# Gated linear attention and feed-forward on eight cores: the copy of y moved to VectorE, three LayerNorm tiles ahead of the loop

## The chip, the cores and the metric

The kernel runs on the 8 cores of one Trainium2 chip. Each core works on 2,048 of 16,384 tokens, without talking to the others. The metric is the device time of the slowest core in microseconds (us), the median of several runs.

## What is computed

The reference, cut to what matters (B = 1, T = 16384, D = 1024, 16 heads of 64, hidden size 3072):

```python
xn = layernorm(x)
q, k, v = xn @ Wq.T, xn @ Wk.T, xn @ Wv.T     # split in 16 heads
a = sigmoid(xn @ Wg.T)
h_t = a_t[:, None] * h_{t-1} + k_t[:, None] * v_t[None, :]
y_t = q_t @ h_t
x = x + layernorm(y) @ Wo.T
xm = layernorm(x)
x = x + (silu(xm @ wg.T) * (xm @ wu.T)) @ wd.T   # int32 weights / 127
```

## The kernel before

Every core takes its own 2,048 tokens and 256 tokens ahead of them, from which it warms up the state h. The program writes an instruction list for each engine by hand: `O.add("v", ...)` appends to VectorE's list, `"s"` is ScalarE, `"t"` TensorE, `"g"` GpSimd, `"sy"` SyncE, which issues the transposing DMAs. The lists run in order; between engines only the semaphores named in `wait=` hold: TE, VE, SE, GE count the instructions of TensorE, VectorE, ScalarE and GpSimd, the others DMAs (SX loads of x, ST transposes of the normed x, KT and YT transposes of k and y, GX and XQ residual loads and stores). On VectorE, ScalarE and GpSimd each instruction also waits for the one before it on its own engine.

The attention half goes by groups: a warm-up group of 2 tiles of 128 tokens, then four full groups of 4 tiles (8 chunks of 64 tokens). A group has two parts.

- `finish` (lines 385 to 512) projects v (line 406, copied out at 413), runs the second half of the cumulative sums of the log gates (scans, line 435), takes exponentials (443, 446) and projects q and k (475), which line 491 scales.
- `emit_loop` (lines 520 to 778) runs over the chunks, two to a window w. A chunk has the score matmuls (628) into PSUM `p_py`, the mask (641) on VectorE, the state matmuls (651), and `emit_update` (665): lines 667, twice, and 678 on VectorE. At the end of a window TensorE computes y for both chunks (705, 715) into `p_py`. Four copies (731) bring y to `s_y`; SyncE transposes it (744); `emit_update` for the odd chunk follows; then pieces of the next group's front are woven in; then `emit_yln` computes the LayerNorm statistics of y on ScalarE (258 to 277); and `emit_be_late(w - 1)` makes the output projection of the window before (575) with its VectorE work (590, 596, 600, twice each). GpSimd copies half of v across partitions for the next window (557, 561).

The pieces woven in are the `units` that `prep_front` makes for the next group: four LayerNorm tiles on ScalarE (`u_tile`, lines 258 to 284), the transposes (`u_xt`, line 321, four DMAs), eight blocks of the gate projection (`u_gblk`: line 339 on TensorE, 345 and 349 on ScalarE), and the first half of the scans (`u_scan0`, line 360). The table `sched` says how many are taken in each window: 5, 4, 4, 0, and the rest after window 3. The last group has no successor and an empty list. `pyf` holds the count at which a bank of `p_py` is free again.

After the attention half come a second LayerNorm over 16 tiles (lines 845 to 882, transposed at 875 into `s_x2T`), and the feed-forward stage: lines 910 and 923 for gate and up, 949 for down. Line 885 loads all down weights, then line 895 the first gate weights, both on GpSimd's queue.

The table is this line:

```python
sched = {4: [5, 4, 4, 0], 2: [6, 7]}[npair]
```

Of the kernel before, what the change touches and what calls it, by code (L numbers as in the profile page):

```python
# [10 lines left out]
AF = mybir.ActivationFunctionType  # L11
# [6 lines left out]
C = 64  # L18
# [57 lines left out]
def build_program():  # L76
# [73 lines left out]
    ST = _Sem(nc.alloc_semaphore("ST"))  # L150
    KT = _Sem(nc.alloc_semaphore("KT"))
    YT = _Sem(nc.alloc_semaphore("YT"))
    GQ = _Sem(nc.alloc_semaphore("GQ"))
# [5 lines left out]
    VE = _Sem(nc.alloc_semaphore("VE"))  # L159
    SE = _Sem(nc.alloc_semaphore("SE"))  # L160

    O = _Ops()
# [52 lines left out]
    for j in range(8):  # L215
# [4 lines left out]
            wait=([(TE, bw_te)] if j == 0 else ()), inc=VE)  # L220
# [7 lines left out]
    pyf = {0: 0, 1: 0}  # L228
# [4 lines left out]
    G = dict(st_last=0,  # L233
             y_last=0,
             qk_te=0,
             e_wo_te=0,
             fr_se={},
             ln1_se={},
             xr_store={},
             fr_ve={},  # L240
             e_wo_te2=0,
             scan0_ve=0, e0_done=0,
             yt_slot={},
# [48 lines left out]
    def prep_front(tb, nt, wu, gp2):  # L292
# [92 lines left out]
        def finish(dbg_this=False):  # L385
# [7 lines left out]
            def first_use(bk):  # L393
                if bk < 2:
                    return [(VE, pv[0])]
                if bk < 4:
                    return [(SE, pyf[bk - 2])]
                return [(SE, G["fr_se"].get(bk - 4, 0)),
                        (VE, G["fr_ve"].get(bk - 4, 0))]

# [119 lines left out]
    def emit_loop(tb, nt, wu, FR, splice, dbg_this=False):  # L520
# [30 lines left out]
        xr_load(1)  # L551
        if splice:
            splice.loads()
        vsg = {}

        def emit_vs(w2):
# [59 lines left out]
        for cc in range(nch):  # L616
# [7 lines left out]
            if not wu:  # L624
                for h in range(NH):
                    hp, hq = h % 2, h // 2
                    O.add("t", lambda t, w=w, h=h, hp=hp, hq=hq, par=par, cc=cc:
                          t.matmul(
                        p_py[64 * hp:64 * (hp + 1),
                             512 * par + 64 * hq:512 * par + 64 * (hq + 1)],  # L630
                        s_kt[64 * hp:64 * (hp + 1),
                             1024 * w + TILE * hq + C * par:
                             1024 * w + TILE * hq + C * (par + 1)],
                        s_qt[64 * hp:64 * (hp + 1),
                             512 * hq + C * cc:512 * hq + C * (cc + 1)],
                        start=True, stop=True),
                        wait=([(VE, FR["qk_done"]), (SE, pyf[par])]
                              if h == 0 else ()),
                        inc=(TE if h == NH - 1 else None))
                p_mm_done = TE.n  # L640
                O.add("v", lambda v, par=par: v.tensor_tensor(  # L641
                    s_P[:, 512 * par:512 * (par + 1)],
                    p_py[:, 512 * par:512 * (par + 1)],
                    s_mask[:, 512 * par:512 * (par + 1)], ALU.mult),
                    wait=[(TE, p_mm_done)], inc=VE)
                pmask_done = VE.n
# [41 lines left out]
            if (not wu) and par == 1:  # L688
                ug = max(upd_ve.get((gc[0] - 1) % 3, 0),
                         upd_ve.get(gc[0] % 3, 0))  # L690
                for c2 in (cc - 1, cc):
                    par2 = c2 % 2
                    hs2 = (gc[0] - (cc - c2)) % 3
                    for h in range(NH):
                        hp, hq = h % 2, h // 2
                        rhs_v = (
                            (lambda t, c2=c2, hp=hp, h=h:
                             s_V[64 * hp:64 * (hp + 1),
                                 1024 * (c2 // 2) + 64 * h:1024 * (c2 // 2) + 64 * (h + 1)])
                            if hp == par2 else  # L700
                            (lambda t, hp=hp, h=h:
                             s_VS[64 * hp:64 * (hp + 1), 64 * h:64 * (h + 1)])
                        )
                        O.add("t", lambda t, c2=c2, par2=par2, h=h, hp=hp, hq=hq,
                              rhs_v=rhs_v: t.matmul(  # L705
                                  p_py[64 * hp:64 * (hp + 1),
                                       512 * par2 + 64 * hq:512 * par2 + 64 * (hq + 1)],
                                  s_P[64 * hp:64 * (hp + 1),
                                      512 * par2 + 64 * hq:512 * par2 + 64 * (hq + 1)],
                                  rhs_v(t),  # L710
                                  start=True, stop=False),
                              wait=(([(VE, max(pmask_done, ug)), (GE, vs_done)])
                                    if h == 0 else ()))
                        O.add("t", lambda t, c2=c2, par2=par2, h=h, hp=hp, hq=hq,
                              hs2=hs2: t.matmul(  # L715
                                  p_py[64 * hp:64 * (hp + 1),
                                       512 * par2 + 64 * hq:512 * par2 + 64 * (hq + 1)],
                                  s_qt[64 * hp:64 * (hp + 1),
                                       512 * hq + C * c2:512 * hq + C * (c2 + 1)],
                                  s_h[hs2][64 * hp:64 * (hp + 1),  # L720
                                           64 * hq:64 * (hq + 1)],
                                  start=False, stop=True),
                              inc=(TE if (h == NH - 1 and c2 == cc) else None))
                G["y_last"] = TE.n
                vsu[0] = TE.n
                if w + 1 < npair:
                    emit_vs(w + 1)
                for par2 in (0, 1):
                    for hp in (0, 1):
                        O.add("s", lambda s, ysl=ysl, par2=par2, hp=hp:  # L730
                              s.activation(  # L731
                            s_y[64 * par2:64 * (par2 + 1),
                                ysl:ysl + 1024].rearrange(
                                "p (q two o) -> p q two o", two=2, o=C)[:, :, hp, :],
                            p_py[64 * hp:64 * (hp + 1),
                                 512 * par2:512 * (par2 + 1)].rearrange(
                                "p (q o) -> p q o", o=C),
                            AF.Copy),
                            wait=(([(TE, TE.n),
                                    (YT, G["yt_slot"].get(w % 2, 0))])  # L740
                                  if (par2 == 0 and hp == 0) else ()),
                            inc=SE)
                    pyf[par2] = SE.n
                O.dma("sy", YT, lambda sy, w=w, ysl=ysl: sy.dma_start(
                    out=s_E[:].rearrange("p (j q c) -> p j q c",
                                         j=8, q=4, c=TILE)[:, :, w, :],
                    in_=s_y[:, ysl:ysl + 1024].rearrange(
                        "p (j c) -> p j c", j=8),
                    transpose=True),
                    wait=[(SE, SE.n)])  # L750
                yt_eps[w] = O.close_epoch(YT)
                G["yt_slot"][w % 2] = yt_eps[w]
                emit_update()
                if splice:
                    sched = {4: [5, 4, 4, 0], 2: [6, 7]}[npair]
                    for _ in range(min(sched[w], len(splice))):
                        splice.pop(0)()
                yst[w] = emit_yln(w)
                G["yst_slot"][w % 2] = yst[w]
                if w > 0:  # L760
                    emit_be_late(w - 1)
                if splice and w == npair - 1:
                    while splice:
                        splice.pop(0)()
            elif splice and wu and par == 1:
                sched = {2: [6, 7]}[npair]
                for _ in range(min(sched[w], len(splice))):
                    splice.pop(0)()
                if w == npair - 1:
                    while splice:  # L770
                        splice.pop(0)()
# [69 lines left out]
        O.add(eng, fn, wait=w, inc=sem, inc_by=16)  # L841

    a2_done = {}
    ln2q = {}
    for tt in range(16 if TRUNC == 0 else 0):
        buf = tt % 2
        dmaD("g", GX, lambda g, tt=tt, buf=buf: g.dma_start(
# [29 lines left out]
                                   j=8, q=16, c=TILE)[:, :, tt, :],  # L877
            in_=s_a2[:].rearrange("p (j c) -> p j c", j=8), transpose=True),
            wait=[(VE, a2_done[tt])])
        if tt % 4 == 3:  # L880
            ln2q[tt // 4] = O.close_epoch(ST)
    ln2_tp = ST.n

    if TRUNC == 0:
# [8 lines left out]
    for hc in range(NHC if TRUNC == 0 else 0):  # L893
# [10 lines left out]
        gu_ld = O.close_epoch(GQ)  # L904
        for t4 in range(4):
            pb = t4 % 2
            w0 = [(GQ, gu_ld), (ST, ln2q.get(t4, ln2_tp)),
                  (SE, silu_of.get(pb, 0))]
            for j in range(8):
                addD("t", lambda t, buf=buf, t4=t4, j=j, pb=pb: t.matmul(  # L910
                    p_g[pb][:],
# [128 lines left out]
```

How the kernel before makes its waits and increments, by code:

```python
        def run(e, fn=fn, w=w, inc=inc, inc_by=inc_by):  # L56
            for sem, val in w:
                e.wait_ge(sem.h, val)
            ins = fn(e)
            if inc is not None and ins is not None:
                ins.then_inc(inc.h, inc_by)
# [931 lines left out]
        @block.gpsimd  # L993
        def _(g):
            for f in O.q["g"]:
                f(g)
            g.wait_ge(XQ.h, final_xq)
            if final_dq:
                g.wait_ge(DQ.h, final_dq)
```

## Time and profile before

| | |
|---|---|
| runs | 1534.56 and 1540.17 us, median 1537.36 us |
| profiled execution | 1543.56 us, span of its slowest core (core 3) 1542.0 us |
| spans of the eight cores | 1518.9 to 1542.0 us |
| busy in the span | TensorE 956.0 us, VectorE 469.3, ScalarE 368.6, GpSimd 136.2 |
| loops of the four full groups begin at | 285.6, 459.5, 637.6 and 814.3 us |
| second LayerNorm, feed-forward | from 892.9, from 1032.1 us |

The profile is of one execution, times are counted from the first instruction of core 3. Busy time says little here: the attention half is a chain in which engines wait for each other, so the questions are what TensorE waits for, and what stands ahead of that in its queue. Names in the profile are engine, line, output tile and input tiles; a bracket at a row's end is the idle time of the engine ahead of it and what ended it. PE is TensorE, DVE is VectorE, ACT is ScalarE, POOL is GpSimd, SPq the queue of SyncE.

### The profile page before, as it was taken

To read this page: it belongs to the slowest core of one execution; us is meant where nothing else is said; L and a number is where in the kernel's file an instruction comes from. 1 tells how busy PE (TensorE), PEld (TensorE's weight loads), DVE (VectorE), ACT (ScalarE), POOL (GpSimd) and SP (SyncE) were. 2 spreads that over 40 slices of the span, in tenths; PEclk is the share of its full clock that TensorE was granted. 3 is DMA by queue.
4 is the path that set the end of the run, shared out by engine and by line. 5 is a ranking of instruction groups with operands and counts; after the bars stand their busy time and mean duration, and the time that the engine had idled before them with its cause. 6 is when DMAs were issued, how large, how long until landed. Compare 5 with 4: busy or idle time off the path is not lost.

```text
span 1542.0 us, 17776 instructions; the slowest of 8 cores (1518.9 to 1542.0 us)
## 1 busy us (share of the span) xinstructions
PE 956.0 (62%) x5892; PEld 450.5 (29%) x5892; DVE 469.3 (30%) x864; ACT 368.6 (24%) x755; POOL 136.2 (9%) x193
## 2 busy tenths in 40 slices
PE   0115178635762666725675500029999999999997
PEld 0003133313322332413233200004444444444443
DVE  0023235405742266404655534201122111111111
ACT  0032521274106531174203322101111111100000
POOL 2000000101101001001001000001011110101100
PEclk9967576667885777657886755559999999999999
DMA  9902400212201212211103246882444434403232
GB/s 142 164 11 85 78 18 0 36 35 69 99 25 28 63 48 96 35 35 48 63 14 56 68 123 141 149 119 29 41 42 41 39 31 41 55 28 107 93 101 96
DMA packets 144457, 99.98 MB, mean 65 GB/s; under 512 B 123504, under 2 KB 123504, under 8 KB 144368
## 3 DMA queue, kind: packets, MB, share of 16 engines
q0 software_dynamic: 72816, 81.02, 25.6%
q1 hardware_dynamic: 71552, 17.83, 6.5%
q8 instruction: 49, 0.80, 0.2%
q14 instruction: 40, 0.33, 0.1%
HBM read 93.86 MB, written 16.78 MB: 72 GB/s over the span
## 4 chain that ended last, share of the span: by engine, by line
PE 51%; DVE 16%; ACT 11%; DMA 10%; issue 5%; another core or an unknown queue 5%; DVEq 1%; SPq 1%; ACTq 0%; POOL 0%; POOLq 0%
PE p_g L910 11%; PE p_u L923 11%; PE p_d L949 11%; PE p_fr L339 5%; DMA s_x2T<-s_a 4%; PE p_pp L575 3%; DVE s_nL L360 3%; DMA s_wd<-wdi 3%; DVE s_nL L435 3%; PE p_py L475 3%; PE p_fr L475 2%; ACT s_nL L258 2%; ACT s_nL L261 2%; DVE p_pp L590 2%
## 5 line engine op out<-in xcount | busy, mean ns | idle before, releaser
L910 PE MATMUL p_g<-s_x2T,s_wgu 128*128 128x512 bf16 x768 | 183.1, 382 | 149.7 <-DMA s_wgu<-wui 149.7
L923 PE MATMUL p_u<-s_x2T,s_wgu 128*128 128x512 bf16 x768 | 182.4, 381 | 0.0
L339 PE MATMUL p_fr<-s_xlnT,s_wg 128*128 128x512 bf16 (+1 forms) x320 | 83.7, 428 | 146.2 <-ACT s_y L731 82.8
L949 PE MATMUL p_d<-s_wd,s_hff 128*128 128x512 bf16 x768 | 165.9, 379 | 1.2 <-DVE s_hff L929 1.2
L929 DVE SCALAR_TENSOR_TENSOR s_hff<-p_u,s_act 128x512 bf16<-128x512 f32 x96 | 66.4, 692 | 295.6 <-PE p_u L923 295.6
L910 PEld LDWEIGHTS p_g<-s_x2T,s_wgu 128*128 128x128 bf16 x768 | 75.4, 98 | 241.6 <-issue 151.9
L916 ACT ACTIVATE s_act<-p_g 128x512 f32<-128x512 f32 x96 | 57.3, 597 | 271.1 <-PE p_g L910 271.1
L923 PEld LDWEIGHTS p_u<-s_x2T,s_wgu 128*128 128x128 bf16 x768 | 75.4, 98 | 91.7 <-issue 1.9
L949 PEld LDWEIGHTS p_d<-s_wd,s_hff 128*128 128x128 bf16 x768 | 75.1, 98 | 92.0 <-issue 1.7
L339 PEld LDWEIGHTS p_fr<-s_xlnT,s_wg 128*128 128x128 bf16 x320 | 34.7, 113 | 191.6 <-issue 178.1
L575 PE MATMUL p_pp<-s_wo,s_E 128*128 128x512 bf16 x256 | 76.7, 467 | 21.3 <-DVE s_xr L600 21.3
L731 ACT ACTIVATE s_y<-p_py 64x512 bf16<-64x512 f32 x64 | 37.9, 592 | 212.4 <-PE p_py L715 207.1
L590 DVE SCALAR_TENSOR_TENSOR p_pp<-p_pp,s_stats,s_bwB 128x512 f32<-128x512 f32 x32 | 24.3, 758 | 198.8 <-PE p_pp L575 131.8
L705 PE MATMUL p_py<-s_V,s_P 64*64 64x64 bf16 x256 | 29.8, 237 | 80.6 <-DVE s_P L641 80.6
L360 DVE TENSOR_TENSOR_SCAN s_nL<-s_S 128x64 f32<-128x64 bf16 x160 | 46.7, 292 | 69.7 <-ACT s_S L349 52.3
L667 DVE TENSOR_TENSOR s_ht<-p_st,s_h 64x512 f32<-64x512 f32 x72 | 49.6, 688 | 59.2 <-PE p_st L651 51.9
L956 DVE TENSOR_TENSOR s_x<-s_x,p_d 128x1024 f32<-128x1024 f32 x16 | 19.5, 1221 | 148.1 <-PE p_d L949 148.1
L475 PE MATMUL p_py<-s_xlnT,s_wq 128*128 128x512 bf16 x128 | 40.2, 484 | 36.2 <-DVE s_qt L491 36.2
L406 PE MATMUL p_py<-s_wv,s_xlnT 128*128 128x512 bf16 x144 | 42.7, 463 | 22.8 <-DVE s_V L413 22.8
L705 PEld LDWEIGHTS p_py<-s_V,s_P 64*64 64x64 bf16 x256 | 28.2, 151 | 82.1 <-issue 82.1
L183 PE MATMUL p_pp<-s_wo,s_betT 128*1 128x512 bf16 x16 | 4.9, 474 | 72.2 <-DMA s_onec<-ones_c 72.2
L895 POOL DMA_DIRECT2D s_wgu<-wgi x24 | 21.0, 874 | 314.1 <-PE p_u L923 214.4
(109 smaller groups left out, 1137.8 us busy)
## 6 DMA issues: line engine op xcount, KB each, us to landing
s_x<-x2d POOLq DMA_DIRECT2D x32, 512.0 KB, 4.7
s_x<-xs POOLq DMA_DIRECT2D x18, 512.0 KB, 8.8
s_xr<-xs POOLq DMA_DIRECT2D x16, 512.0 KB, 4.5
x2d<-s_xr POOLq DMA_DIRECT2D x16, 512.0 KB, 2.9
out<-s_x POOLq DMA_DIRECT2D x16, 512.0 KB, 3.0
s_wd<-wdi POOLq DMA_DIRECT2D x1, 6144.0 KB, 46.4
s_wgu<-wgi POOLq DMA_DIRECT2D x24, 256.0 KB, 4.5
s_wgu<-wui POOLq DMA_DIRECT2D x24, 256.0 KB, 5.3
```

Of the source, the lines that this page charges most:

```text
L339: O.add("t", lambda t, p=p, j=j, bank=bank: t.matmul(p_fr[bank][:, 0:ntok], s_wg[:, 1024 * j + TILE * p:1024 * j + TILE * (p + 1)], s_xlnT ...
L360: O.add("v", lambda v, cc=cc, p=p: v.tensor_tensor_scan(s_nL[:, 512 * cc + C * p:512 * cc + C * (p + 1)], s_S[:, 512 * p + C * cc:512 * p ...
L475: ntok=ntok: t.matmul(bank6(bank, ntok), s_w[:, 1024 * j + TILE * p:1024 * j + TILE * (p + 1)], s_xlnT[:, 512 * j:512 * j + ntok], start=( ...
L575: O.add("t", lambda t, w=w, j=j, hf=hf: t.matmul(p_pp[hf][:], s_E[:, 512 * j + TILE * w:512 * j + TILE * (w + 1)], s_wo[:, 1024 * j + 512 ...
L590: v.scalar_tensor_tensor(p_pp[hf][:], p_pp[hf][:], r_ap, s_bwB[:, sl], ALU.mult, ALU.add),
L667: O.add("v", lambda v, par=par, hp=hp, hs=hs: v.tensor_tensor(s_ht[64 * hp:64 * (hp + 1), :].rearrange("p (q o) -> p q o", o=C), p_st[64 * ...
L705: rhs_v=rhs_v: t.matmul(p_py[64 * hp:64 * (hp + 1), 512 * par2 + 64 * hq:512 * par2 + 64 * (hq + 1)], s_P[64 * hp:64 * (hp + 1), 512 * par ...
L910: addD("t", lambda t, buf=buf, t4=t4, j=j, pb=pb: t.matmul(p_g[pb][:], s_wgu[buf][:, TILE * j:TILE * (j + 1)], s_x2T[:, 2048 * j + 512 * t ...
L916: addD("s", lambda s, pb=pb: s.activation(s_act2[:], p_g[pb][:], AF.Silu, scale=SCL), wait=[(TE, TE.n), (VE, hff_of.get(1 - pb, 0))], inc=SE)
L923: addD("t", lambda t, buf=buf, t4=t4, j=j, pb=pb: t.matmul(p_u[pb][:], s_wgu[buf][:, 1024 + TILE * j:1024 + TILE * (j + 1)], s_x2T[:, 2048 ...
L929: addD("v", lambda v, hc=hc, t4=t4, pb=pb: v.scalar_tensor_tensor(s_hff[:, 2048 * hc + 512 * t4:2048 * hc + 512 * (t4 + 1)], p_u[pb][:], S ...
L949: addD("t", lambda t, ts=ts, buf=buf, hf=hf, hcc=hcc: t.matmul(p_d[buf][:, 512 * hf:512 * (hf + 1)], s_hff[:, 2048 * hcc + TILE * ts:2048 ...
```

## The change

- The four copies of line 731 become `tensor_copy` on VectorE (line 733 after). They count on VE; the score matmuls, the projection of v and the transpose of y wait for VE in place of SE. The first copy of a window also waits for ScalarE's statistics of the window two before, since those read the `s_y` that it overwrites.
- Three units are taken from the list before the loop of a group begins: the first three LayerNorm tiles. The table takes three fewer in window 0, so all others stay where they were.
- The first gate matmul of each quarter in the feed-forward stage waits for all 16 transposes of the second LayerNorm; it used to wait for those of its own quarter. The epoch of ST is closed at every tile.

```diff
                 if bk < 4:
-                    return [(SE, pyf[bk - 2])]
+                    return [(VE, pyf[bk - 2])]
...
         if splice:
             splice.loads()
+            for _ in range(min(3, len(splice) - 9)):
+                splice.pop(0)()
...
-                        wait=([(VE, FR["qk_done"]), (SE, pyf[par])]
+                        wait=([(VE, max(FR["qk_done"], pyf[par]))]
...
-                        O.add("s", lambda s, ysl=ysl, par2=par2, hp=hp:
-                              s.activation(
+                        O.add("v", lambda v, ysl=ysl, par2=par2, hp=hp:
+                              v.tensor_copy(
...
-                                "p (q o) -> p q o", o=C),
-                            AF.Copy),
+                                "p (q o) -> p q o", o=C)),
                             wait=(([(TE, TE.n),
-                                    (YT, G["yt_slot"].get(w % 2, 0))])
+                                    (YT, G["yt_slot"].get(w % 2, 0)),
+                                    (SE, G["yst_slot"].get(w % 2, 0))])
                                   if (par2 == 0 and hp == 0) else ()),
-                            inc=SE)
-                    pyf[par2] = SE.n
+                            inc=VE)
+                    pyf[par2] = VE.n
...
-                    wait=[(SE, SE.n)])
+                    wait=[(VE, VE.n)])
...
-                    sched = {4: [5, 4, 4, 0], 2: [6, 7]}[npair]
+                    sched = {4: [2, 4, 4, 0], 2: [3, 7]}[npair]
...
-        if tt % 4 == 3:
-            ln2q[tt // 4] = O.close_epoch(ST)
+        O.close_epoch(ST)
...
-            w0 = [(GQ, gu_ld), (ST, ln2q.get(t4, ln2_tp)),
-                  (SE, silu_of.get(pb, 0))]
+            w0 = [(GQ, gu_ld), (ST, ln2_tp), (SE, silu_of.get(pb, 0))]
```

ScalarE at the head of a full group's loop, before. Line 446 is the last exponential of `finish`, `s_x` in lines 258 and 261 a LayerNorm tile of the next group:

```order
L443 ACTIVATE s_E<-s_nL 128x2048
L446 ACTIVATE s_Er<-s_nL 128x2048
L731 ACTIVATE s_y<-p_py 64x8x64 x4
L258 ACTIVATE s_nL,s_stats<-s_x 128x1024
L261 ACTIVATE s_nL,s_stats<-s_x 128x1024
```

The same place after the change:

```order
L443 ACTIVATE s_E<-s_nL 128x2048
L446 ACTIVATE s_Er<-s_nL 128x2048
L258 ACTIVATE s_nL,s_stats<-s_x 128x1024
L261 ACTIVATE s_nL,s_stats<-s_x 128x1024
L263 ACTIVATE s_stats<-s_stats 128x1
```

The copy of y of window 0 is gone, and the LayerNorm tiles follow the exponentials; all four stand in a row, as they did behind the copy, and the statistics of y of window 0 behind them.

VectorE in windows 0 and 1 of the same group, before, from the first mask (641) to the second window's first mask:

```order
L641 TENSOR_TENSOR s_P<-p_py,s_mask 128x512
L667 TENSOR_TENSOR s_ht<-p_st,s_h 64x512 x2
L678 TENSOR_TENSOR s_h<-s_ht,s_ec 128x512
L641 TENSOR_TENSOR s_P<-p_py,s_mask 128x512
L667 TENSOR_TENSOR s_ht<-p_st,s_h 64x512 x2
L678 TENSOR_TENSOR s_h<-s_ht,s_ec 128x512
L641 TENSOR_TENSOR s_P<-p_py,s_mask 128x512
```

After, with the line numbers of the changed file, two higher here:

```order
L643 TENSOR_TENSOR s_P<-p_py,s_mask 128x512
L669 TENSOR_TENSOR s_ht<-p_st,s_h 64x512 x2
L680 TENSOR_TENSOR s_h<-s_ht,s_ec 128x512
L643 TENSOR_TENSOR s_P<-p_py,s_mask 128x512
L733 CAST s_y<-p_py 64x8x64 x4
L669 TENSOR_TENSOR s_ht<-p_st,s_h 64x512 x2
L680 TENSOR_TENSOR s_h<-s_ht,s_ec 128x512
L643 TENSOR_TENSOR s_P<-p_py,s_mask 128x512
```

The four copies stand between the mask of the odd chunk and its state update, which is now behind them. The lists of TensorE, SyncE and GpSimd keep their order.

## Rows read from the trace of the kernel before

**Rows 1.** List of waits: engine, line, releaser; us in total, times, longest.
```profile
PE p_fr L339 <- ACT s_y L731: 82.8, 3, 27.9
```
**Rows 2.** Timeline of TensorE, second full group: start us, us, line, count.
```profile
506.69 9.75 PE L339 MATMUL p_fr<-s_xlnT,s_wg 128*128 128x512 bf16 x32 [27.89 <-ACT s_y L731]
...
535.72 4.00 PE L339 MATMUL p_fr<-s_xlnT,s_wg 128*128 128x512 bf16 x16 [0.42 <-ACT s_S L349]
```
**Rows 3.** Timeline of ScalarE, 433 to 507 us.
```profile
435.16 1.91 ACT L446 ACTIVATE s_Er<-s_nL 128x2048 bf16<-128x2048 f32 x1
470.44 2.64 ACT L731 ACTIVATE s_y<-p_py 64x512 bf16<-64x512 f32 x4 [33.38 <-PE p_py L715]
...
497.63 1.24 ACT L284 ACTIVATE s_xln<-s_x,s_stats 128x1024 bf16<-128x1024 f32 x1
498.96 1.06 ACT L258 ACTIVATE s_nL<-s_y 128x1024 f32<-128x1024 bf16 x1
...
504.35 2.64 ACT L731 ACTIVATE s_y<-p_py 64x512 bf16<-64x512 f32 x4
```
**Rows 4.** Timeline of SyncE's queue, same group: start and length of issuing.
```profile
473.22 1.22 SPq L744 DMA_TRANSPOSE s_E<-s_y  x1
499.05 5.18 SPq L321 DMA_TRANSPOSE s_xlnT<-s_xln  x4
```
**Rows 5.** Line 321 over the whole span, 18 transposes.
```profile
DMA to landing us min/median/max: 2.8/3.0/12.8
```
**Rows 6.** Line 302, the loads of s_x: one group's issue, and all 18.
```profile
414.91 2.08 POOL L302 DMA_DIRECT2D s_x<-xs  x4
...
DMA to landing us min/median/max: 5.9/8.8/65.1
```
**Rows 7.** Groups of instructions by line: busy us, mean ns of one; idle before.
```profile
L413 DVE CAST s_V<-p_py 128x512 bf16<-128x512 f32 x18 | 12.4, 692 | 13.3 <-PE p_py L406 12.3
```
**Rows 8.** Timeline of VectorE, window 0 of the second full group.
```profile
467.10 0.69 DVE L641 TENSOR_TENSOR s_P<-p_py,s_mask 128x512 bf16<-128x512 f32 x1
467.89 1.49 DVE L667 TENSOR_TENSOR s_ht<-p_st,s_h 64x512 f32<-64x512 f32 x2
469.49 0.69 DVE L678 TENSOR_TENSOR s_h<-s_ht,s_ec 128x512 bf16<-128x512 f32 x1
472.68 0.69 DVE L641 TENSOR_TENSOR s_P<-p_py,s_mask 128x512 bf16<-128x512 f32 x1 [2.50 <-PE p_py L628]
```
**Rows 9.** Timeline of VectorE, window 3 of the same group.
```profile
560.14 0.76 DVE L590 SCALAR_TENSOR_TENSOR p_pp<-p_pp,s_stats,s_bwB 128x512 f32<-128x512 f32 x1 [4.70 <-PE p_pp L575]
...
565.17 1.08 DVE L360 TENSOR_TENSOR_SCAN s_nL<-s_S 128x64 f32<-128x64 bf16 x3
```
**Rows 10.** Timeline of VectorE, last group, first line 590 in windows 1 and 2.
```profile
838.49 0.76 DVE L590 SCALAR_TENSOR_TENSOR p_pp<-p_pp,s_stats,s_bwB 128x512 f32<-128x512 f32 x1 [4.93 <-PE p_pp L575]
...
855.12 0.76 DVE L590 SCALAR_TENSOR_TENSOR p_pp<-p_pp,s_stats,s_bwB 128x512 f32<-128x512 f32 x1 [5.36 <-PE p_pp L575]
```
**Rows 11.** GpSimd's first copy (timeline), and VectorE beside both copies (chain).
```profile
418.88 1.04 POOL L557 COPY s_VS<-s_V 64x1024 bf16<-64x1024 bf16 x1 [1.88 <-DVE s_V L413]
...
419.12 0.95 DVE s_nL L435
...
420.16 1.07 DVE s_nL L435
```
**Rows 12.** Windows: us, busy (count) of five engines, granted TensorE clock, DMA share, GB/s.
```profile
470.00:480.00 10.00, 4.78 (x128) 4.55 (x128) 5.70 (x9) 8.18 (x18) 3.07 (x3) 0.50 0.13 30
...
506.50:509.00 2.50, 2.31 (x6) 0.87 (x7) 0.00 (x0) 0.49 (x1) 0.00 (x0) 0.50 0.34 78
```
**Rows 13.** SyncE's last transposes of the second LayerNorm, and the chain behind.
```profile
977.13 8.56 SPq L875 DMA_TRANSPOSE s_x2T<-s_a  x2
...
978.62 46.39 DMA s_wd<-wdi
...
1026.51 5.30 DMA s_wgu<-wui
```

More of the change, by code:

```diff
@@ L765, in emit_loop @@
             elif splice and wu and par == 1:
-                sched = {2: [6, 7]}[npair]
+                sched = {2: [3, 7]}[npair]
                 for _ in range(min(sched[w], len(splice))):
@@ L843, in build_program @@
     a2_done = {}
-    ln2q = {}
     for tt in range(16 if TRUNC == 0 else 0):
```

## The prediction

> **What bounds the kernel now.** I read the list of waits first. Between the warm-up and the feed-forward stage one long wait of TensorE stands out that this change can touch: line 339, the gate projection of the next group, waits 82.8 us in 3 waits and is released by ScalarE's line 731, the copy of y out of PSUM [rows 1]. Three waits, because three of the four full groups prepare a successor.
>
> Then the timelines of the second full group. TensorE stands idle 27.9 us before its 32 matmuls of line 339 at 506.69 [rows 2]. ScalarE explains it [rows 3]: done with the exponentials at 437.07 it idles until y of window 0 is ready at 470.44, copies it, and only then runs four LayerNorm tiles of the next group (to 498.87), the statistics of y, and the copy of y of window 1 at 504.35. So 25.8 us of LayerNorm that depend on nothing in this loop stand behind a copy that does, and the transposes of their result are issued at 499.05 [rows 4]. The page names the copy at 504.35 as releaser, but line 339 waits for ST (the transposes) and for bank semaphores that were raised long ago; the last transpose is the true gate, 7.64 us after 499.05. In this stage no engine is at its limit: it is one chain of latencies, and what counts is where each link stands in its queue.
>
> **The change part by part.**
>
> 1. Three LayerNorm tiles go ahead of the loop, and line 731 leaves ScalarE. Both are needed: with no copy of y in front, the fourth tile, which the schedule still pops at window 0, follows the third at once. Four tiles take 498.87 − 473.18 = 25.7 us (the first begins where the copy ended, 470.44 + 2.64 + 0.10), so from 437.1 they end at 462.8, inside ScalarE's old idle time. Their input was issued at 414.91 over 2.08 us and lands after 8.8 us as a rule, by 426 [rows 6]. The tiles cost nothing where they now stand; the cover is 33.4 us of idle ScalarE.
>
> What is late next? Two things, in the second group:
> - SyncE. Its order is kept: the transpose of y of window 0 (1.22 us), then four of line 321 [rows 4]. y is ready on VectorE at about 470.4; four copies later, 473.6, the first is issued (0.14 us after, as before); line 321 starts at 475.0, and with the same 7.64 us line 339 can start at 482.6.
> - TensorE, which has window 1's y ahead of line 339. VectorE now does, in a row: mask (ends 467.8), the copies from 470.4, the update (2.29 us with its gaps, formerly done while TensorE computed y [rows 8]), and then window 1. Copies 4 × 0.79 = 3.16, update 2.39: the next mask stands at 475.95, where it stood at 472.68, 3.3 us late. Mask, update, mask (3.8) end at 479.8, and y takes until 482.3 (2.65 us from mask to evacuation, as 467.79 to 470.44).
>
> The two meet at 482.6 instead of 506.69: 24.1 us gained. The idle time of 27.9 so loses all but 3.8, and over three groups that is 82.8 − 3 × 3.8 = **71.4 us**.
>
> 2. The price of one copy on VectorE. The trace has no such copy of 64x512, so I bound it: line 413, the same kind of copy over 128 partitions, takes 692 ns [rows 7], and two of line 667, 64 partitions out of PSUM with the same stride, 1.49 us with the gap between them [rows 8]; I take 0.69 and 0.10 between two, as everywhere on VectorE. Lower end: 0.59, what ScalarE took. Upper end: 0.76, the scalar_tensor_tensor of line 590 [rows 9]. 36 copies lie on the path (below), so the ends are −4 and +3 us.
>
> 3. Window 2. ScalarE no longer makes the exponential wait for a copy: the stall of 0.42 us goes in the second group [rows 2], **−0.4**. Copies and update (5.55 us) lie beside 12 us of TensorE work there.
>
> 4. Window 3. Formerly the update ran beside y, and VectorE then idled 4.70 us for the output projection [rows 9]. Copies and update now fill 5.55 us of it: 0.9 late. Behind that, y's statistics are waited on by the scans of line 360, and they now start after the update, at 561.2; 5.3 us later (the statistics stand from 498.96 to just before 504.35 [rows 3]) is 566.5, with a semaphore 566.6, against 565.17: 1.4 us late. Three groups: **+4.2**.
>
> 5. The last group has no LayerNorm tiles to gain from and pays in full. Window 0: 3.3 late, as above. Then VectorE had 4.93 and 5.36 us of idle time before line 590 in windows 1 and 2 [rows 10], and a little more in window 3; 5.55 us of copies and update overrun it by 0.6, 0.2 and 0. Together **+4.1**.
>
> 6. Sets on the path: window 0 and 3 in three groups, windows 0 to 2 in the last: 9 sets, 36 copies.
>
> 7. The start of the feed-forward stage now waits for all second-LayerNorm transposes and not for a quarter of them. The last is issued by 985.7, while the weights of line 895 follow the 46.39 us load of s_wd and land at 1031.8 [rows 13]. Cost 0; cover 40 us. Closing an epoch at every tile adds a wait on SyncE that VectorE's own wait before line 871 has already served: 0. The warm-up group has no copy of y, and its queues read the same in both kernels: 0. The third semaphore on the first copy (statistics of two windows ago) is served some 30 us before: 0; if it were late, update and output residual would queue behind it.
>
> **Sum:** −71.4 − 0.4 + 4.2 + 4.1 = −63.5 us. The profiled execution took 1543.56 us (1.6 of it outside its span), so 1480.1; it was 0.4% above the median of the runs, 1537.36, and the same ratio of 0.9589 makes 1474.1 of that. I say 1474 us.
>
> **Rivals.**
>
> *A. GpSimd and VectorE get in each other's way.* GpSimd's two copies of s_VS begin when y is done, exactly where the four copies now stand. The trace shows such a meeting: during them two scans of 0.30 us took 0.95 and 1.07 [rows 11], 1.4 us lost. If the new copies suffer alike, it costs 1.4 us in the six sets with a GpSimd copy beside them (window 0 in three groups, windows 0 to 2 in the last): +9, 1483 us; the most is the whole 2.1 us of both, +12. Against it: the scan reads SBUF, the copy reads PSUM and only writes SBUF. The Trainium skill ("SBUF — State Buffer", Who interferes with whom) says that a VectorE instruction with two SBUF inputs contends with a GpSimd one that reads SBUF, and that one with at most one SBUF input, outside the two-port modes, does not; by that rule the trace's scans agree and the new copies go free.
>
> *B. The clock of TensorE.* The 32 matmuls of line 339 began at a granted clock of 0.50, 1.2 GHz [rows 12], and took 9.75 us; in window 2, 16 took 4.00 [rows 2]. If the shorter idle time leaves the clock up, window 1 goes at 8.0: 3 × 1.75 = 5 us more gain, 1469. Against it: the clock was at 0.50 already from 470 to 480, while TensorE ran 128 of the small matmuls. The Trainium skill ("TensorE: Matmul & The Clock Gate", What's actually happening) has idling lower the clock and activity raise it; by that alone removing an idle stretch should help, but the row of 470 to 480 says the stretch that stays is slow too.
>
> *C. The transposes land late.* They now run close behind y's transpose and with GpSimd's traffic. They landed after 3.0 us, at most 12.8 [rows 5]. At 12.8 each time it costs 3 × 9.8 = 29 us: 1503.
>
> *D. Slower.* The LayerNorm tiles are held by their input. The s_x loads landed after 8.8 us, but once after 65.1 [rows 6]. If in the steady groups they land 56 us after issue or later, at 473 or beyond, the four tiles stand where they stood, nothing of part 1 is gained, and the copies' 4.2 + 4.1 remain: 1537.4 + 8 = 1545. Up to 32 us the forecast is untouched. Against it: the DMA engines are little used here (a share of 0.13 from 470 to 480 [rows 12]), and 65.1 fits the first loads, queued behind the weights.
>
> **How the numbers follow.** Forecast 0.80 (its own range 1464 to 1484: the copies' ends, and some us for semaphore gaps), A 0.07, B 0.05, C 0.05, D 0.03. The range takes in A and B and most of C: 1460 to 1497. A difference of 2% is about what a measurement of this kernel can tell from no change; 2% below is 1506.6. All of forecast, A, B and most of C lie below: 0.93. Within 2%: D and the rest of C, 0.06. Slower: 0.01.
>
> **What would show it.** Right: ScalarE runs four LayerNorm tiles straight behind line 446; the wait of line 339 falls from 27 to under 2 us; line 321 is issued right after the transpose of window 0's y; one copy takes 0.69 us. Wrong: copies of 1 us or more beside GpSimd (A); line 321's landing over 6 us (C); ScalarE idle before line 258 for SX (D). The forecast fails if another wait fills the 24 us, which I could then read as the releaser of line 339.

## The result and the profile after

The changed kernel was timed twice. The first set gave a ratio of 0.9647 to the kernel before (95% interval 0.9615 to 0.968), the second 0.9613 (0.960 to 0.9626), that is 1476.3 us beside 1536.4. The prediction was 1474.0, by its own sum a ratio of 0.959. The median over all runs of the first set, 1488.0 us, holds runs in which cores had a lower clock; the ratios leave those out.

The profiled execution took 1489.1 us, and core 2 was its slowest:

```profile
core 2: 1487.5 us, clock 0.810
core 3: 1479.1 us, clock 0.814
core 4: 1479.9 us, clock 0.810
```

The list of waits of the changed kernel answers to [rows 1]:

```profile
PE p_fr L339 <- DMA s_xlnT<-s_xln: 60.6, 3, 30.1
PE p_fr L339 <- DVE s_y L733: 3.8, 2, 1.9
```

The 82.8 us in three waits are gone. What is left of them is 3.8 us in two, and a small one of 1.7 us among the DMA waits; the rest of that row is two waits of some 30 us at the start of the program, which stood there before. ScalarE's timeline says why, second full group, to compare with [rows 3]:

```profile
405.34 1.91 ACT L446 ACTIVATE s_Er<-s_nL 128x2048 bf16<-128x2048 f32 x1
407.34 1.06 ACT L258 ACTIVATE s_nL<-s_x 128x1024 f32<-128x1024 f32 x1
...
412.46 1.24 ACT L284 ACTIVATE s_xln<-s_x,s_stats 128x1024 bf16<-128x1024 f32 x1
...
432.09 1.24 ACT L284 ACTIVATE s_xln<-s_x,s_stats 128x1024 bf16<-128x1024 f32 x1
...
445.56 1.06 ACT L258 ACTIVATE s_nL<-s_y 128x1024 f32<-128x1024 bf16 x1 [12.23 <-DVE s_h L680]
```

Four LayerNorm tiles run from 407.34 to 433.33, 0.09 us behind line 446, and ScalarE then idles until y's statistics. SyncE's queue, in the places of [rows 4], TensorE's first line 339 ([rows 2]), and how long line 321 took to land, over the whole span ([rows 5]) and, in the second row, in this group alone:

```profile
443.10 1.23 SPq L746 DMA_TRANSPOSE s_E<-s_y  x1
444.53 5.31 SPq L321 DMA_TRANSPOSE s_xlnT<-s_xln  x4
```
```profile
453.43 9.43 PE L339 MATMUL p_fr<-s_xlnT,s_wg 128*128 128x512 bf16 x32 [1.93 <-DVE s_y L733]
```
```profile
DMA to landing us min/median/max: 2.7/4.3/12.6
...
DMA to landing us min/median/max: 2.7/2.8/4.4
```

Read against the start of its own loop (429.53, the issue of line 524), line 339 starts 23.9 us in. Before it was 506.69 − 459.45 = 47.2. So 23.3 us are gained in this group, where the prediction had 24.1. The row names the copy as releaser. But the last transpose, issued at 448.5, was the one that took 4.4 us: it landed at 452.9, and line 339 began 0.5 us behind it. Before the change the last one was issued at 503.0, took 3.2 us, and line 339 began 0.5 us behind that too. The landing is the true gate in both: the column tells the last semaphore event that the profile could match, not always the last condition.

VectorE in windows 0 and 1, in the place of [rows 8]:

```profile
436.72 0.69 DVE L643 TENSOR_TENSOR s_P<-p_py,s_mask 128x512 bf16<-128x512 f32 x1
439.90 3.06 DVE L733 CAST s_y<-p_py 64x512 bf16<-64x512 f32 x4 [2.49 <-PE p_py L717]
443.06 1.49 DVE L669 TENSOR_TENSOR s_ht<-p_st,s_h 64x512 f32<-64x512 f32 x2
444.66 0.69 DVE L680 TENSOR_TENSOR s_h<-s_ht,s_ec 128x512 bf16<-128x512 f32 x1
445.46 0.69 DVE L643 TENSOR_TENSOR s_P<-p_py,s_mask 128x512 bf16<-128x512 f32 x1
```

Four copies last 3.06 us. VectorE idles 2.49 us for y, and the update, which ran in that idle time before, now stands behind the copies.

The groups one by one, on core 4 of each profiled execution. It is chosen because no group of it ran slower than its fellows in the profile of before; in us, from one start of the loop to the next, and the last group to the second LayerNorm. The rows from `copies_only` on are the experiments below; the first set's profile has a lower granted clock in groups 1 and 2 (0.71 and 0.74) than that of core 3 (0.78 and 0.77):

| kernel | groups 1, 2, 3 | last group | ratio (95%) |
|---|---|---|---|
| before | 173.5, 173.9, 174.1 | 87.4 | 1 |
| changed, first set | 157.8, 154.4, 152.4 | 93.6 | 0.9647 (0.9615 to 0.968) |
| changed, second set | 153.7, 150.6, 153.3 | 93.6 | 0.9613 (0.960 to 0.9626) |
| copies_only | 150.4, 150.6, 153.3 | 93.2 | 0.9595 (0.9555 to 0.9634) |
| held | 176.1, 174.5, 174.2 | 93.1 | 1.0058 (1.0038 to 1.0077) |
| act3 | 154.1, 156.5, 154.1 | 87.0 | 0.9626 (0.960 to 0.9652) |
| act4 | 150.7, 150.0, 150.4 | 87.0 | 0.9536 (0.9504 to 0.9569) |
| act5 | 147.0, 146.6, 147.0 | 86.9 | 0.9454 (0.9431 to 0.9477) |
| after5 | 150.3, 150.3, 150.3 | 93.1 | 0.9581 (0.956 to 0.9601) |
| lastact | 153.8, 150.6, 153.3 | 87.2 | 0.9575 (0.9549 to 0.9601) |
| double | 157.5, 160.0, 157.4 | 103.3 | 0.979 (0.9763 to 0.9816) |
| upd_first | 150.3, 150.3, 153.6 | 87.4 | 0.9564 (0.955 to 0.9577) |
| weave | 140.6, 142.8, 143.6 | 87.1 | 0.9381 (0.9368 to 0.9394) |

### The profile page after: what moved, and what is told of

Read it like the earlier page. It is cut to its first block, busy times and chain, and to the rows that moved or that the text cites. A ratio compares the mean times of both kernels' runs of the same rounds, so it can differ in the third digit from the quotient of the medians.

```text
span 1487.5 us, 17772 instructions; the slowest of 8 cores (1469.8 to 1487.5 us)
## 1 busy us (share of the span) xinstructions
PE 957.9 (64%) x5892; PEld 450.6 (30%) x5892; DVE 513.5 (35%) x928; ACT 330.7 (22%) x691; POOL 136.0 (9%) x193
## 4 chain that ended last, share of the span: by engine, by line
PE 53%; DVE 19%; DMA 10%; ACT 5%; issue 5%; another core or an unknown queue 5%; SPq 1%; DVEq 1%; ACTq 0%; POOL 0%; POOLq 0%
PE p_d L948 12%; PE p_g L909 11%; PE p_u L922 11%; PE p_fr L339 5%; DMA s_x2T<-s_a 4%; DVE s_nL L360 3%; DVE s_nL L435 3%; DMA s_wd<-wdi 3%; PE p_py L475 3%; DVE s_ht L669 2%; DVE s_y L733 2%; PE p_fr L475 2%; PE p_pp L577 2%; PE p_py L406 2%
## 5 line engine op out<-in xcount | busy, mean ns | idle before, releaser
L948 PE MATMUL p_d<-s_wd,s_hff 128*128 128x512 bf16 x768 | 185.3, 410 | 1.2 <-DVE s_hff L928 1.2
L909 PEld LDWEIGHTS p_g<-s_x2T,s_wgu 128*128 128x128 bf16 x768 | 75.4, 98 | 240.3 <-issue 150.6
L948 PEld LDWEIGHTS p_d<-s_wd,s_hff 128*128 128x128 bf16 x768 | 79.6, 104 | 106.8 <-issue 65.0
L733 DVE CAST s_y<-p_py 64x512 bf16<-64x512 f32 x64 | 44.1, 688 | 44.9 <-PE p_py L717 40.0
L258 ACT ACTIVATE s_nL<-s_y 128x1024 f32<-128x1024 bf16 x16 | 16.9, 1057 | 151.5 <-DVE s_h L680 150.9
```

Of the source, the lines that this page charges most:

```text
L733: v.tensor_copy(s_y[64 * par2:64 * (par2 + 1), ysl:ysl + 1024].rearrange("p (q two o) -> p q two o", two=2, o=C)[:, :, hp, :], p_py[64 * h ...
L909: addD("t", lambda t, buf=buf, t4=t4, j=j, pb=pb: t.matmul(p_g[pb][:], s_wgu[buf][:, TILE * j:TILE * (j + 1)], s_x2T[:, 2048 * j + 512 * t ...
L948: addD("t", lambda t, ts=ts, buf=buf, hf=hf, hcc=hcc: t.matmul(p_d[buf][:, 512 * hf:512 * (hf + 1)], s_hff[:, 2048 * hcc + TILE * ts:2048 ...
```

## The experiments

Edits are shown against the changed kernel or the kernel before, as said; `...` marks code left out, and the warm-up group's own line of the table, changed alike each time, is not shown. They test two claims: that the gain is where the LayerNorm tiles stand and nothing else, and that the copies on VectorE cost some 8 us that need not be paid.

**Only the copies are moved** (`copies_only`, against the changed kernel):

```diff
-            for _ in range(min(3, len(splice) - 9)):
-                splice.pop(0)()
...
-                    sched = {4: [2, 4, 4, 0], 2: [3, 7]}[npair]
+                    sched = {4: [5, 4, 4, 0], 2: [6, 7]}[npair]
```

> The changed kernel without the pops ahead of the loop, with the old table (5, 4, 4, 0): only the copies are on VectorE. Theory: window 0's copies were all that stood between line 446 and the LayerNorm tiles in ScalarE's list, so the pops change no list and this takes the time of the changed kernel, some 1482 us beside 1538 (ratio 0.965); the four tiles run straight behind line 446 and the wait of line 339 stays near 2 us. Rival (as the prediction words it, 'both are needed'): without the pops the tiles stay where they were, and only the copies' price is left, some 1546 us (1.005).

It gave 0.9595, and ScalarE does the same as in the changed kernel; the rows are core 4's in this run:

```profile
402.17 1.91 ACT L446 ACTIVATE s_Er<-s_nL 128x2048 bf16<-128x2048 f32 x1
404.17 1.06 ACT L258 ACTIVATE s_nL<-s_x 128x1024 f32<-128x1024 f32 x1
```

Once the copies are off ScalarE, the pops ahead of the loop change nothing: what the table calls "window 0" is, in ScalarE's list, the head of the loop.

**Three tiles ahead of the loop, copies on ScalarE** (`act3`, against the kernel before):

```diff
             splice.loads()
+            for _ in range(min(3, len(splice) - 9)):
+                splice.pop(0)()
...
-                    sched = {4: [5, 4, 4, 0], 2: [6, 7]}[npair]
+                    sched = {4: [2, 4, 4, 0], 2: [3, 7]}[npair]
```

> The kernel before with three tiles popped ahead of the loop (table 2, 4, 4, 0), the copies still on ScalarE. Theory: three tiles are done at some 457 us in the second full group, the fourth waits behind the copies of y (470.4 to 473.1) and ends at 479.7, so the gate blocks start at 487.5 in place of 506.7: 3 x 19.2 = 57.6 us off, and nothing is added to VectorE: 1480 us beside 1538 (0.963), as good as the changed kernel. L339 then waits some 8.7 us a group, for L321. Rival: the gain needs the copy on VectorE; then this stays at 1538 (1.00).

0.9626, 1478.3 us. ScalarE, SyncE and TensorE of core 4, second full group, loop from 435.27:

```profile
431.10 1.24 ACT L284 ACTIVATE s_xln<-s_x,s_stats 128x1024 bf16<-128x1024 f32 x1
445.50 2.64 ACT L733 ACTIVATE s_y<-p_py 64x512 bf16<-64x512 f32 x4 [13.16 <-PE p_py L717]
448.24 1.06 ACT L258 ACTIVATE s_nL<-s_x 128x1024 f32<-128x1024 f32 x1
```
```profile
454.77 5.29 SPq L321 DMA_TRANSPOSE s_xlnT<-s_xln  x4
```
```profile
462.66 9.35 PE L339 MATMUL p_fr<-s_xlnT,s_wg 128*128 128x512 bf16 x32 [8.79 <-DMA s_xlnT<-s_xln]
```

Three tiles lie ahead of the copy and the fourth behind it, ending at 454.6. Line 339 starts 27.4 us after the loop's start, a wait of 8.8 where 8.7 was expected. The pops alone earn what the whole change earns.

**Four tiles, copies on ScalarE** (`act4`): as act3 with `min(4, ...)` and the table 1, 4, 4, 0.

> As act3 with all four tiles ahead of the loop (table 1, 4, 4, 0), copies on ScalarE. Theory: gate blocks start at some 482 us as in the changed kernel, and the 8.3 to 10 us that the copies cost VectorE in window 3 and in the last group are not paid: 8 to 10 us under the changed kernel, some 1472 us beside 1538 (0.957); the last group is back at 87.2 us from 93.5. Rival (part of the gain comes from the copies on VectorE themselves, as ScalarE's copies wait behind its statistics): no better than the changed kernel, 0.965 or above.

0.9536, 1464.9 us: 11.4 us under the changed kernel's second set, more than both intervals and a little more than the 8 to 10 expected; the last group is 87.0. But here line 321 has become the wait (core 3):

```profile
459.47 3.15 PE L339 MATMUL p_fr<-s_xlnT,s_wg 128*128 128x512 bf16 x7 [4.74 <-DMA s_xlnT<-s_xln]
```

**Line 321 ahead of the loop too** (`act5`): as act4 with `min(5, ...)` and the table 0, 4, 4, 0.

> As act4 with the transposes of the normed x (line 321) ahead of the loop too (table 0, 4, 4, 0), copies on ScalarE. In act4 TensorE ended window 1's y at 454.7 us and idled 4.74 us for line 321, which had been issued behind the transpose of window 0's y. Theory: with line 321 issued as soon as the fourth tile is done (439.7) it lands before window 1's y ends, the wait is gone: 3 x 4.7 = 14 us under act4's 1465, some 1451 us (0.944). Rival (the time goes elsewhere: the 32 matmuls of line 339 then run at the low clock, or the transposes of k and y queue behind line 321): within 3 us of act4, 0.951 or above.

0.9454, 1453.3 us: 11.7 us under act4 of the 14 expected. Core 0, loop from 424.40:

```profile
429.92 6.15 SPq L321 DMA_TRANSPOSE s_xlnT<-s_xln  x4
```
```profile
443.73 8.22 PE L339 MATMUL p_fr<-s_xlnT,s_wg 128*128 128x512 bf16 x31 [0.34 <-DVE s_h L680]
```

Line 339 no longer waits. Neither the transposes of k nor that of y are held up.

**The same with the copies on VectorE** (`after5`, against the changed kernel: `min(5, ...)`, table 0, 4, 4, 0).

> The changed kernel with all four tiles and line 321 ahead of the loop (table 0, 4, 4, 0), copies on VectorE. In the changed kernel TensorE idles only 0.6 to 1.8 us before line 339, because VectorE, with the copies, brings window 1's y later. Theory: 3 x 0.6 to 1.8 = 2 to 5 us off the changed kernel, ratio 0.958 to 0.961; against act5 it is 10 to 20 us longer, since VectorE bounds the windows. Rival (the copies cost the same 8 us wherever they stand): act5 plus 8 us.

0.9581, 1471.7 us, 4.6 off the changed kernel (their intervals still touch) and 18.4 over act5, where they are far apart. The rival's 8 us is refuted: with line 339's wait gone, what the copies add to VectorE (3.3 to 3.7 us in a steady group, by the table) is no longer hidden behind it, and the last group's 6.2 come on top.

**The copies on VectorE without their effect on the tiles** (`held`, against the changed kernel):

```diff
-                              64 + 16 * tt, [(SX, ep), (ST, xt_ep.get(0, 0))])
+                              64 + 16 * tt, [(SX, ep), (ST, xt_ep.get(0, 0)),
+                                             (VE, G.get("copies_ve", 0))])
...
                     pyf[par2] = VE.n
+                G["copies_ve"] = VE.n
```

with no pops ahead of the loop and the old table. Every LayerNorm tile of a group so waits for window 0's copies.

> Copies on VectorE, but the first LayerNorm tile of a group waits for the copies of window 0, so that ScalarE's tiles stand where they stood. Theory: the gate blocks start at some 507 us again, the gain of 71 us is gone and the price of the copies is left alone: the sum gives 1537.4 + 8.3 = 1546, with the 2 us more that the last group showed 1548 (1.005 to 1.007). Rival (the copies on VectorE shorten windows by themselves, or cost much more than 8 us in the spliced windows 1 and 2): under 1530, or over 1560.

1.0058, 1545.1 us: +8.9 us by the ratio (5.8 to 11.8), where the sum had +8.3. ScalarE and TensorE of core 4, loop from 455.41, line 339 being line 340 here:

```profile
469.40 1.06 ACT L258 ACTIVATE s_nL<-s_x 128x1024 f32<-128x1024 f32 x1 [36.58 <-DVE s_y L732]
```
```profile
502.53 9.88 PE L340 MATMUL p_fr<-s_xlnT,s_wg 128*128 128x512 bf16 x32 [24.80 <-DMA s_xlnT<-s_xln]
```

One wait put back on ScalarE takes the whole gain away. This is the prediction's case D made by hand, which had 1545.

**The last group's copies back on ScalarE** (`lastact`, against the changed kernel; a branch on `not splice` emits the copies of before, and the scores from the third chunk on and the transpose wait for SE):

```diff
+        last = not splice
...
+                if last:
+                            O.add("s", lambda s, ysl=ysl, par2=par2, hp=hp:
+                                  s.activation(
...
+                        pyf[par2] = SE.n
```

> The changed kernel with the last group's copies back on ScalarE; the three groups before keep them on VectorE. Theory: in the last group nothing is woven in, ScalarE is free and VectorE is the bound, so the group falls from 93.5 us to the 87.2 us of before: 6.3 us off the changed kernel, ratio 0.958; by the prediction's term 4.1 us. Rival (the last group's growth comes from something else than the copies on VectorE): no change, 0.962.

0.9575, 1470.7 us, 5.5 off the changed kernel by intervals that just touch; the table is clearer: the last group is back at 87.2 while the others keep their times: its growth is the copies', whole.

**Every copy made twice** (`double`, against the changed kernel: `for rep, par2 in ((0, 0), (1, 0), (0, 1), (1, 1))`, eight copies a window).

> The changed kernel with every copy of y made twice (8 casts a window, 3.1 us more on VectorE each). Theory: in the steady groups windows 0 and 3 and in the last group all four windows pay it, windows 1 and 2 hide it beside TensorE's gate blocks: (3 x 2 + 4) x 3.1 = 31 us over the changed kernel, ratio 0.982. Rival (VectorE bounds all 16 windows): 16 x 3.1 = 50 us, ratio 0.994.

0.979 against 0.9613: 0.0177 × 1536 = 27 us, for 31 expected and 50 by the rival. In the table (against the changed kernel's second set) the last group grew by 9.7 and the steady ones by 3.8, 9.4 and 4.1. In the last group four times 3.17 us would be 12.7. Windows 2 and 3 pay it in full (6.3 us), windows 0 and 1 together 5.6; the rest is made up behind them, 0.9 us in the last output projection, whose first matmuls take 5.38 us here for 6.28, and 1.3 in the wait for the second LayerNorm's first input. The count of paying windows (10, not 16) is borne out in sum; the steady groups, unequal among themselves, don't say which of their windows pay.

**The update ahead of the copies** (`upd_first`, against the changed kernel):

```diff
+                emit_update()
                 for par2 in (0, 1):
...
                 G["yt_slot"][w % 2] = yt_eps[w]
-                emit_update()
```

> The changed kernel with the odd chunk's state update (2.4 us on VectorE) ahead of the copies of y, where it runs beside TensorE's y matmuls as in the kernel before. Theory: what costs in the last group is mostly that the update moved behind the copies; the group falls from 93.3 us to some 88 us (before 87.2): 5 us there, and 0 to 1.5 us in each steady group: 5 to 9 us off the changed kernel, ratio 0.954 to 0.957. Rival (the copies' own time is the cost): 2 us or less off.

0.9564, 1468.4 us, 7.9 off the changed kernel with every copy still on VectorE; the last group is 87.4. VectorE of core 4 in window 1 of the last group:

```profile
755.88 1.49 DVE L669 TENSOR_TENSOR s_ht<-p_st,s_h 64x512 f32<-64x512 f32 x2 [0.47 <-DVE s_P L643]
757.48 0.69 DVE L680 TENSOR_TENSOR s_h<-s_ht,s_ec 128x512 bf16<-128x512 f32 x1
758.28 3.06 DVE L734 CAST s_y<-p_py 64x512 bf16<-64x512 f32 x4
762.32 0.76 DVE L592 SCALAR_TENSOR_TENSOR p_pp<-p_pp,s_stats,s_bwB 128x512 f32<-128x512 f32 x1 [0.98 <-PE p_pp L577]
```

The update now fills the 2.5 to 2.8 us in which VectorE waited for y, the copies follow without a gap, and VectorE idles again before the output projection. The price of the copies was the order on VectorE more than the copies.

**The feed-forward's wait restored** (`after_ln2q`, against the changed kernel: `ln2q` filled at every fourth tile and used in `w0` as in the kernel before), and the changed kernel again (`after_again`), in one set:

> The changed kernel with the feed-forward's wait for the transposes of each quarter restored. Theory: the weights of line 895 gate the stage some 40 us behind the last transpose, so the wait costs nothing: the changed kernel's time within 2 us (0.1%). Rival: the wait for all 16 tiles holds the first gate matmul; then this is several us faster.

> The changed kernel again. Its first set gave a ratio of 0.965 (0.9615 to 0.968), the same lists in the run with the old table 0.9595 (0.9555 to 0.963), the prediction's sum 0.959. If the sum is right this gives 0.957 to 0.963; if 0.965 was the kernel's own value, 0.963 to 0.967.

0.9603 (0.9586 to 0.962) and 0.9613 (0.960 to 0.9626): no difference shows. In `after_again` the weights are what the stage waits for; the list of waits of its core 4 has

```profile
PE p_g L909 <- DMA s_wgu<-wui: 154.1, 1, 154.1
```

**A gate block in TensorE's idle time** (`weave`, against act5):

```diff
+            if (not wu) and par == 1 and splice and w in (1, 2):
+                splice.pop(0)()
             if (not wu) and par == 1:
...
-                    sched = {4: [0, 4, 4, 0], 2: [1, 7]}[npair]
+                    sched = {4: [0, 3, 3, 0], 2: [1, 7]}[npair]
```

> act5 with one gate block (line 339, 8 matmuls, 2 us) taken ahead of window 1's and window 2's y, where TensorE idles 2.4 to 3.8 us for the mask, and one fewer behind (table 0, 3, 3, 0). Theory: each fills idle time, 3 groups x 2 x 2 us = up to 12 us off act5's 1453, some 1441 us (0.938). Rival (the block comes late for the mask, or ScalarE's and VectorE's parts bound the window): no better than act5, 0.945 or more.

0.9381, 1441.7 us, 11.6 off act5's 1453.3, the 12 of the theory. TensorE of core 2, window 1: the first block stands ahead of y, the rest behind it, and the waits between them are short.

```profile
434.74 3.19 PE L339 MATMUL p_fr<-s_xlnT,s_wg 128*128 128x512 bf16 x7 [0.33 <-issue]
439.25 3.40 PE L339 MATMUL p_fr<-s_xlnT,s_wg 128*128 128x512 bf16 x15 [0.18 <-issue]
443.98 1.89 PE L339 MATMUL p_fr<-s_xlnT,s_wg 128*128 128x512 bf16 x8 [1.33 <-ACT s_S L349]
```

This version computes the reference in full and beats both kernels: 95 us under the kernel before, 35 under the changed one.

## Why the prediction was right, step by step

**Part 1, the released gate, −71.4.** Right in cause and nearly in size. The gate moved by 23.3 us for 24.1. The wait itself fell further, from 27.9 to 1.9, since window 1's y, which stands ahead of line 339, now ends 2.6 us later behind the copies. The prediction calls 3.8 us the idle time that is left; it is the part of the old wait by which the gate did not move, and the sum is right with it. `held` shows that the whole gain hangs on ScalarE's tiles, and act3 and act4 reach it without touching VectorE. What failed is the sentence "Both are needed". For the changed kernel the pops are superfluous (copies_only); for the gain the copies' move is (act3, act4). Either edit would have done. I had shown from the lists that all four tiles stand in a row, but had not looked at the list with one edit alone.

**Part 2, the copy at 0.69 + 0.10.** Right. Four last 3.06 us; the groups of the changed kernel have

```profile
L733 DVE CAST s_y<-p_py 64x512 bf16<-64x512 f32 x64 | 44.1, 688 | 44.9 <-PE p_py L717 40.0
```

**Parts 3 and 4, windows 2 and 3, −0.4 and +4.2.** On core 4 the three steady groups of before sum to 521.5, those of the second set to 457.7: 63.8 us gained for −71.4 − 0.4 + 4.2 = −67.6. In copies_only it is 67.2. `held` has +2.6, +0.6 and +0.1 in the three groups, 3.3 us where windows 0 to 3 would give 4.2. The terms of single windows can't be told from this: some groups come out some 3 us apart in one kernel (150.4 on core 0 and 153.7 on core 4, both the first full group of the second set; the last section has what the traces say of it).

**Part 5, the last group, +4.1.** The term that was mis-sized: it measured +6.2 (87.4 to 93.6), and lastact gives it all back. From the timelines of core 4, before and second set:

```profile
830.17 0.76 DVE L590 SCALAR_TENSOR_TENSOR p_pp<-p_pp,s_stats,s_bwB 128x512 f32<-128x512 f32 x1 [4.96 <-PE p_pp L575]
...
868.74 5.27 PE L575 MATMUL p_pp<-s_wo,s_E 128*128 128x512 bf16 x16 [5.32 <-DVE s_xr L600]
...
874.25 0.76 DVE L590 SCALAR_TENSOR_TENSOR p_pp<-p_pp,s_stats,s_bwB 128x512 f32<-128x512 f32 x1 [5.66 <-PE p_pp L575]
```
```profile
766.18 0.76 DVE L592 SCALAR_TENSOR_TENSOR p_pp<-p_pp,s_stats,s_bwB 128x512 f32<-128x512 f32 x1
...
805.12 6.28 PE L577 MATMUL p_pp<-s_wo,s_E 128*128 128x512 bf16 x16 [6.03 <-DVE s_xr L602]
...
812.00 0.76 DVE L592 SCALAR_TENSOR_TENSOR p_pp<-p_pp,s_stats,s_bwB 128x512 f32<-128x512 f32 x1 [7.02 <-PE p_pp L577]
```

The first output projection's line 592 comes 27.97 us after the group's first mask (738.21), before 23.45 after it (806.72): windows 0 and 1 cost 4.5, for 3.3 + 0.6. Windows 2 and 3 cost 0.4 for 0.2. And the last output projection, which the prediction left out, costs 1.4: its first 16 matmuls take 6.28 us where they took 5.27, after an idle time of 6.03 in place of 5.32. No wait was missed there but a speed: both began at half clock, and the second stayed there longer. Two windows of each, of core 4 before and of the second set, with the granted clock as third number from the end:

```profile
870.00:872.00 2.00, 2.00 (x6) 0.71 (x5) 0.00 (x0) 0.00 (x0) 0.00 (x0) 0.50 0.64 262
872.00:875.00 3.00, 2.01 (x9) 0.69 (x7) 0.75 (x1) 0.00 (x0) 0.00 (x0) 0.98 0.00 0
```
```profile
806.50:808.50 2.00, 2.00 (x7) 0.62 (x6) 0.00 (x0) 0.00 (x0) 0.00 (x0) 0.50 0.64 262
808.50:811.50 3.00, 2.90 (x9) 0.94 (x7) 0.00 (x0) 0.00 (x0) 0.00 (x0) 0.66 0.00 0
```

The second rows begin 3.3 and 3.4 us behind the first of the matmuls; one was granted 0.98, the other 0.66 in the mean. This is no accident of one execution: on cores 0, 4 and 6 the same 16 matmuls take 5.2 to 5.3 us behind 5.3 us of idle time in before, lastact, upd_first and act5, and 6.1 to 6.3 behind 6.0 to 6.2 in both sets of the changed kernel, copies_only and held. But the length of the idle time is not what decides: in double it is 8.5 to 8.7 us on every core, and the 16 matmuls take 5.2 to 5.4.

**Part 7, the feed-forward's wait, 0.** after_ln2q finds no difference; its interval allows some 3 us.

**Sum.** −63.5 was predicted; the second set's ratio makes −59.5. On core 4 the steady groups fell 3.8 short of their terms and the last group 2.1, together 5.9; over the whole program the shortfall is 4.0. On core 4 the difference is the warm-up group: it took 122.8 us before and 118.8 in the second set, where the prediction had no change. Over the cores of before that group takes from 115.6 to 125.8 us, so no run shows that the change shortens it, and some of the good fit of the total is luck.

**Rivals.** A: GpSimd's copy ran from 439.78 beside the casts of 439.90, and every one of the 64 casts on core 2 took between 681 and 695 ns; refuted. The Trainium skill ("SBUF — State Buffer", Who interferes with whom) says that only the port pair that both engines share contends; the casts, with their input in PSUM, agree. B: in the row above line 339's 32 matmuls took 9.43 us for 9.75, 0.3 and not 1.75. But in the same execution the first full group of core 3 has

```profile
300.57 7.68 PE L339 MATMUL p_fr<-s_xlnT,s_wg 128*128 128x512 bf16 x32 [0.56 <-DMA s_xlnT<-s_xln]
```

and in the second set four groups with 0.5 to 0.6 us of idle time ahead took 8.3 to 8.5 us, one of the others 8.6 and the rest 9.2 to 9.9. In act5, where TensorE idles 0.34 us ahead of them, 31 took 8.22. So the mechanism acts in a few groups of the changed kernel, where little idle time is left, and the 5 us more did not come. C: the slowest landing of this group was 4.4 us, the slowest in a full group of that core 5.3, under the 6 that was to be its sign; 12.6 belongs to the start. The time from issue to landing still matters, by 2 us of the gate (last section). D: ScalarE began line 258 0.09 us behind line 446, so s_x was in place; held shows that its price had been right.

## What to carry to other kernels

When an engine's list has independent work behind an instruction that waits, ask what each candidate edit does to that list alone: here hoisting the work (act4) and moving the waiting instruction (copies_only) open the same gate, and only the second puts load on a third engine, VectorE. If an instruction is moved to a busy engine, put it behind work of that engine that fits into the wait for its input: with the update ahead of the copies 8 us came back (upd_first) of a price that `held` puts at 9. And when one wait is gone, read which condition is now last (line 321, then y, then the mask): three small steps after the change earned 35 us more.

## What was not expected of the hardware

In the profiled execution of the changed kernel the down-projection stage ran slower on two cores, though all eight run the same dense matmuls there. Windows 1380 to 1400 of cores 2 and 4, columns as in [rows 12]:

```profile
1380.00:1400.00 20.00, 20.00 (x78) 8.27 (x76) 1.22 (x1) 0.00 (x0) 2.13 (x4) 0.81 0.32 106
```
```profile
1380.00:1400.00 20.00, 20.00 (x94) 9.08 (x93) 2.07 (x2) 0.00 (x0) 2.13 (x4) 1.00 0.31 106
```

Core 2 was granted 0.81, between the two levels 0.50 and 1.00, and ended 78 matmuls where core 4 ended 94; core 3 had 0.81 too, and cores 0 and 1 had 1.00. The stage took 192 us on core 3 in place of 174 before, which is why core 3, 14.5 us ahead of core 4 at the second LayerNorm, ended level with it, and core 2, 8.4 us ahead there, was the slowest.
The other surprise is how much the clock makes of a small shift: the 16 matmuls of part 5 took 6.28 us in place of 5.27 behind 0.7 us more of idle time, yet 5.38 behind the 8.5 us of double. A term for this can't be read off the idle time alone; what does decide is open.

Part of the steps of some 3 us between groups of one kernel comes from the landing of line 321. In the first full group of the second set its slowest transpose lands after 2.8 us on cores 0 and 6; there line 339 starts 22.7 us after the loop's start and takes 8.53 us, and the group 150.4. On cores 1 to 5 it lands after 4.3 to 4.7 us, line 339 starts after 24.3 to 24.7, and the group takes 153.7. It is not the whole of it: the second full groups all take 150.4 to 150.7 us, while line 339 takes from 8.3 to 9.9 in them. No run varied this.
